# A two-layer transformer with a mixture of experts: work dealt anew over the turns, rounding on GpSimd, tiles fetched at loaded addresses, results scattered

## The reference

```
x  = x + attn0(ln(x)) + ffn0(ln(x))       # the same ln(x) feeds both
x  = x + attn1(ln(x)) + moe(ln(x))

attn:  16 heads of 8 features, softmax over 512 keys, output product (128 x 128)
ffn0:  h = silu(q(xn) @ q(wg)) * (q(xn) @ q(wu))      # 352 hidden features
       y = q(h) @ q(wd)
q(a):  blocks of 16: scale = max|a| / 6; round a / scale to 0 .5 1 1.5 2 3 4 6; times scale
moe:   g = softmax(relu(xn @ Wr1 + br1) @ Wr2 + br2); two best of 8 experts, weights softmax(g2 / 2)
       out = silu(xn @ Ws1 + bs1) @ Ws2 + bs2          # shared expert, 512 hidden features
       out += w_e * (silu(xn @ We1[e] + be1[e]) @ We2[e] + be2[e])   for the two experts e
```

## Time and profile before

| | |
|---|---|
| runs | 1662.01, 1664.07, 1670.28 us |
| profiled execution | 1662.64 us, span 1660.9 us |
| TensorE busy | 1199.5 us (72%), VectorE 1016.8 (61%), ScalarE 723.0 (44%), GpSimd 375.0 (23%) |
| mean granted TensorE clock | 0.868 |
| turns a1 to a7 | from 208.7 to 1278.5 us, with turns b between |
| last maxima with tiles beside them | 1323.7 to 1455.8 us |
| tiles alone | 1455.8 to 1564.1 us |
| last attention, then the end | 1564.1 to 1602.5, then to 1660.9 us |

### The profile page before, as it was taken

One profiled execution on the slowest core, in us unless ns is written; L12 is line 12 of the kernel. 1 busy time (PEld: TensorE's weight loads), 2 busy tenths in 40 slices (PEclk: granted clock), 3 DMA queues, 4 the chain that ended last, 5 costly groups with the idle time before them and its releaser, 6 DMA issues.

```text
span 1660.9 us, 18766 instructions
## 1 busy us (share of the span) xinstructions
PE 1199.5 (72%) x6747; PEld 522.3 (31%) x6807; DVE 1016.8 (61%) x1596; ACT 723.0 (44%) x921; POOL 375.0 (23%) x395
## 2 busy tenths in 40 slices
PE   2657478877786788777867887787778858888851
PEld 1113123212321332223212321232223246677510
DVE  7855677766676767666766676777685425411122
ACT  1045044644464446444644464446454713233450
POOL 5020111101110111011101110111001344455475
PEclk9668668987898889878987798889989979999985
DMA  4934232133313321432133213331410363455332
GB/s 135 349 149 115 89 99 83 30 111 82 85 30 107 95 76 30 112 94 73 29 109 85 84 30 106 80 86 30 113 34 14 96 159 122 131 149 163 110 104 69
DMA packets 143230, 159.65 MB, mean 96 GB/s; under 512 B 14585, under 2 KB 132546, under 8 KB 141090
## 3 DMA queue, kind: packets, MB, share of 16 engines
q1 hardware_dynamic: 129986, 123.87, 26.7%
q0 software_dynamic: 12208, 34.04, 6.9%
q10 hardware_dynamic: 944, 0.54, 0.1%
HBM read 90.11 MB, written 67.76 MB: 95 GB/s over the span
## 4 chain that ended last, share of the span: by engine, by line
PE 27%; DVE 27%; issue 21%; POOL 9%; ACT 6%; DVEq 6%; DMA 3%; SPq 1%; ACTq 0%; POOLq 0%
DVE nm L959 13%; PE sums L347 5%; ACT ex L695 3%; PE mx L359 3%; PE ring L458 3%; PE mx L329 3%; PE mx L409 2%; PE mx L449 2%; PE ring L433 2%; POOL qs L1361 2%; POOL ks L1361 2%; PE ring L253 2%; POOL xn L1313 2%; DVEq L914 1%; DVEq L873 1%
## 5 line engine op out<-in xcount | busy, mean ns | idle before, releaser
L695 ACT ACTIVATE ex<-mx 128x1024 f32<-128x1024 f32 x512 | 512.4, 1025 | 505.4 <-PE mx L359 503.0
L959 DVE TENSOR_REDUCE nm<-mx 128x2 f32<-128x1024 f32 x512 | 600.6, 1216 | 168.8 <-PE mx L329 165.5
L359 PE MATMUL mx<-qs,ks 74*128 74x512 bf16 (+1 forms) x964 | 316.9, 422 | 104.0 <-DMA qs<-nm_hl 52.6
L347 PE MATMUL sums<-ex,vs 128*18 128x512 f32 x2048 | 304.3, 669 | 5.0 <-ACT pv_sb L699 2.6
L329 PE MATMUL mx<-km,qm 32*128 32x512 bf16 x1024 | 151.5, 431 | 83.2 <-DVE nm L959 54.5
L359 PEld LDWEIGHTS mx<-qs,ks 128*128 128x128 bf16 (+1 forms) x1024 | 78.7, 102 | 404.3 <-issue 234.7
L1304 POOL TENSOR_TENSOR rstd<-veps,minus_half 128x4 f32<-128x4 f32 x16 | 16.6, 1038 | 561.3 <-DVE veps L865 561.3
L1340 POOL DMA_INDIRECT xsort<-xn,pos_i x64 | 62.7, 979 | 238.9 <-DVE pos_i L1046 221.8
L1331 POOL TENSOR_TENSOR parts<-qk_f,parts 128x512 bf16<-128x512 f32 x32 | 36.3, 1154 | 321.0 <-DVE parts L876 321.0
L329 PEld LDWEIGHTS mx<-km,qm 32*128 32x128 bf16 x1024 | 36.9, 93 | 222.4 <-DVE nm L959 97.3
L373 PE MATMUL ring<-ident,pv_sb 128*128 128x128 f32 x128 | 21.9, 298 | 59.1 <-DVE att L975 57.6
(11 more groups left out here) (211 smaller groups left out, 1613.8 us busy)
## 6 DMA issues: line engine op xcount, KB each, us to landing
scratch<-parts SPq DMA_DIRECT2D x128, 256.0 KB, 3.6
ks<-scratch SPq DMA_DIRECT2D x64, 256.0 KB
qs<-scratch SPq DMA_DIRECT2D x64, 256.0 KB
xsort<-hs SPq DMA_DIRECT2D x16, 1024.0 KB, 23.5
qm<-scratch SPq DMA_DIRECT2D x64, 128.0 KB, 2.6
km<-scratch SPq DMA_DIRECT2D x64, 128.0 KB, 2.6
rest<-parts SPq DMA_DIRECT2D x32, 128.0 KB, 3.4
ysort<-qs SPq DMA_DIRECT2D x20, 128.0 KB, 1.8
```

The costliest lines, as they stand in the source:

```text
L347: done = pe.matmul(acc[32 * j:32 * j + 2 * VW, :], values[:, start:start + 2 * VW], ex[:, s % NEX, j, :], start=q == 0 and t == 0, stop=q ...
L359: done = pe.matmul(bank[:, j, :], ks[l][r, h, t * P:(t + 1) * P], qs[l][r, h, :], start=True, stop=True)
L695: act.activation(ex[:, s % NEX, 2 * i:2 * i + 2, :], bank[:, :, :], ACT.Exp, scale=SCALE).then_inc(free, 1)
L959: dve.tensor_reduce(nm[l][:, t, h:h + 2], bank[:, :, :], AX.X, ALU.max, negate=True).then_inc(free, 1)
```

## The change

**A new dealing of the turns.** Many pieces of side work stand in other slots. On VectorE the layer norm statistics of batch b+2 (layer 0) stand in turn b(b) instead of a later turn a; GpSimd's `normalize(0, b+2)` goes with them. `split_qk` is cut in two pieces in two slots; so are the halves of the gates and of the shared expert's hidden product, which had shared a slot. The first half of h is quantised in turn b, the second in turn a. The rounding of x and h goes from VectorE to GpSimd (`round_x`, `round_h`). The high part of `max_rows` is copied by ScalarE. On SP `load_rows(0, b+1, 0)` goes ahead of layer 1's stores.

**Clearing.** `xsort` is cleared by 32 transfers of half the size, issued by ScalarE, one in each slot of turns a0 and b0.

**Tiles.** A row of `xsort` carries two more numbers: the token's number and its first expert. SP fetches weights and tokens by plain DMAs whose first row it loads from `w_row` and `x_row` into a register. VectorE works out, for each tile, where each result row belongs (`y_row`), and GpSimd scatters results by indirect DMA to `y2`, which is in the order of the tokens, one plane for a token's first expert and one for the second (rows of padding go to a region aside). The tiles start six slots later in the last turn (`FIRST_TILE`).

**The end.** `result_rows` is gone, and a batch's results come by two plain DMAs on SP instead of eight gathers.

The diff, cut to its core (the moved comparisons in `work_a` and `work_b` are given by those of VectorE):

```diff
@@ TensorE: tile_in; turn_a
-                pe.wait_ge(xg_in[i % 2], (i // 2 + 1) * 32)
+                pe.wait_ge(xg_in[i % 2], (i // 2 + 1) * 16)
...
-                    else:
-                        tile_step(k)
+                    elif k >= FIRST_TILE:
+                        tile_step(k - FIRST_TILE)
@@ ScalarE
+            def max_rows(l, b, half):
+                layer, batches = rows_before(l, b)
+                wait(act, rows_in[layer][half], batches * N_ROWS)
+                bank = from_ring(("m", l, b, half))
+                act.copy(nm_hl[:, half, 0, :], bank[0:NH // 2, :]).then_inc(high_ready, 1)
+            def clear_rows(i):
+                if i < NZERO:
+                    act.dma_start(xsort[i * ZR * P:(i + 1) * ZR * P, :].rearrange("(p r) c -> p (r c)", p=P),
+                                  hs[:, 0:3, :].rearrange("p c t -> p (c t)")[:, 0:ZR * XW]).then_inc(zero_out, 16)
@@ VectorE
-                if step == 2:
-                    quantize_round(dst, T).then_inc(xq_ready, 1)
...
             def max_rows(l, b, half):
-                layer, batches = rows_before(l, b)
-                wait(dve, rows_in[layer][half], batches * N_ROWS)
                 bank = from_ring(("m", l, b, half))
-                dve.tensor_copy(nm_hl[:, half, 0, :], bank[0:NH // 2, :])
-                dve.drain()
+                dve.wait_ge(high_ready, row_sets.at((l, b, half))[1] + 1)
                 dve.tensor_tensor(nm_hl[:, half, 1, :], ...)
...
             def tile_in(i):
                 bank = from_ring(("T", i))
                 dve.tensor_copy(xgT[i % 2], bank[:, 0:TS]).then_inc(ring_free, 1)
+                dve.tensor_scalar(plane[i % 2][:, :], xg[i % 2][:, :, P + 1], t_exp[:, i:i + 1], float(PLANE), ALU.not_equal, ALU.mult)
+                dve.scalar_tensor_tensor(no_token[i % 2][:, :], xg[i % 2][:, :, P], 0.0, aside[:, i, :], ALU.is_equal, ALU.mult)
+                dve.drain()
+                dve.tensor_tensor(plane[i % 2][:, :], plane[i % 2][:, :], xg[i % 2][:, :, P], ALU.add)
+                dve.drain()
+                dve.tensor_tensor(y_row[:, i, :], plane[i % 2][:, :], no_token[i % 2][:, :], ALU.add).then_inc(y_row_ready, 1)
@@ VectorE: work_a, work_b (places)
-                    for i in range(2):
-                        for step in range(3):
-                            if at == (1 + 3 * i + step + i, "c"):
-                                quantize_h(b, i, step)
+                    if at == (1, "c"):
+                        quantize_h(b, 1, 0)
+                    if at == (7, "c"):
+                        quantize_h(b, 1, 1)
-                    if at == (0, "c"):
-                        norm_stats(0, b + 1)
-                    if at == (4, "c"):
-                        split_qk(0, b + 1)
+                    if at == (3, "c"):
+                        split_first(0, b + 1)
+                    if at == (5, "c"):
+                        split_second(0, b + 1)
...
-                    if at == (12, "b"):
+                    if at == (15, "a"):
                         shared_out(b - 1)
...
+                if b + 2 <= LAST and at == (7, "c"):
+                    norm_stats(0, b + 2)
+                    if at == (13, "c"):
+                        quantize_h(b + 1, 0, 0)
+                    if at == (14, "c"):
+                        quantize_h(b + 1, 0, 1)
@@ GpSimd
+            def round_and_scale(d, n, qsc, done, count):
+                for op in (ALU.add, ALU.subtract):
+                    pool.tensor_tensor(d, d, binade[:, 0:n], op).then_inc(rounded, 1)
+                    pool.wait_ge(rounded, 2 * count + (1 if op == ALU.add else 2))
+                d3 = d.rearrange("p (k q) -> p k q", q=QB)
+                pool.tensor_tensor(d3, d3, per_block(qsc, n), ALU.mult).then_inc(done, 1)
...
-            def fetch_weights(i):
-            def fetch_tokens(i):
-            def fetch_results(b):
+            def scatter_results(i):
+                pool.wait_ge(y_row_ready, i + 1)
+                ring_read(pool, ("TO", i))
                 for h in range(2):
+                    pool.indirect_dma_start(out=y2[:, :], out_offset=bass.IndirectOffsetOnAxis(ap=y_row[:, i, h:h + 1], axis=0),
+                                            in_=yo[i % 2][:, h * P:(h + 1) * P], in_offset=None).then_inc(y_out[i % 2], 16)
@@ SP
+            def fetch_weights(i):
+                first = sp.value_load(w_row[0:1, i:i + 1], min_val=0, max_val=(E - 1) * P)
+                if i >= NW:
+                    sp.wait_ge(ring_full, ring.at(("TO", i - NW))[1] + 1)
+                sp.dma_start(wbuf[i % NW], wmoe[bass.ds(first, P), :]).then_inc(w_in[i % NW], 16)
+            def fetch_tokens(i):
+                first = sp.value_load(x_row[0:1, i:i + 1], min_val=0, max_val=ROWS - TS)
+                if i >= 2:
+                    sp.wait_ge(ring_full, ring.at(("T", i - 2))[1] + 1)
+                    sp.wait_ge(y_row_ready, i - 1)
+                sp.dma_start(xg[i % 2], xsort[bass.ds(first, TS), :].rearrange("(h p) c -> p h c", p=P)).then_inc(xg_in[i % 2], 16)
...
-            for i in range(NZERO):
-                sp.dma_start(xsort[i * 16 * P:(i + 1) * 16 * P, :].rearrange("(p r) c -> p (r c)", p=P),
-                             hs[:, :, :].rearrange("p c t -> p (c t)")).then_inc(zero_out, 16)
             load_rows(0, 0, 0)
...
+                if b + 1 <= LAST:
+                    load_rows(0, b + 1, 0)
                 store_early(1, b)
                 load_max(1, b)
                 store_late(1, b)
-                if b + 1 <= LAST:
-                    load_rows(0, b + 1, 0)
...
+            store_base(LAST - 1)
+            sp.wait_ge(tiles_ready, 1)
+            sp.wait_ge(scattered, 16 * 8 * B)
+            for i in range(NW - 2):
+                fetch_weights(i)
             for i in range(NTILE):
...
+                fetch_tokens(i)
+                if i + NW - 2 < NTILE:
+                    fetch_weights(i + NW - 2)
...
             for b in range(B):
+                for c in range(2):
+                    first = c * PLANE + 1 + b * T
+                    sp.dma_start(yb[b % 2][:, c, :, :], y2[first:first + T, :].rearrange("(t p) c -> p t c", p=P)).then_inc(yb_in[b % 2], 16)
```

More of the change, by code:

```diff
@@ L35 @@
 ROWS = E * CAP
-NZERO = ROWS // (16 * P)
+XW = P + 2
+ZR = 8
+NZERO = ROWS // (ZR * P)
+PLANE = B * T + 1
+FIRST_TILE = 6
 TS = 256
@@ L87, in two_layers @@
 def two_layers(nc, x, w_qkv, w_out0, b_out0, w_gate, w_up, w_down, wqT, wkT, wvT, woT, bq, bk, bv, bo,
-               wr1, br1, wr2, br2, w1s, b1s, w2s, wmoe, b2, scratch, rest, xsort, ysort, base, out):
+               wr1, br1, wr2, br2, w1s, b1s, w2s, wmoe, b2, scratch, rest, xsort, y2, base, out):
     ctx = ExitStack()
@@ L335, in max_rows @@
                     pair_read(pe, ("M", l, b, u, i))
+                row_sets.take((l, b, half))
                 transpose_tiles(("m", l, b, half), lambda t: nm[l][:, t, half * 8:half * 8 + 8], cols=NH // 2)
@@ L633, in _ @@
             turn_a(B)
-            for i in range(SLOTS, NTILE + 1):
-                if i == SLOTS:
+            for i in range(SLOTS - FIRST_TILE, NTILE + 1):
+                if i == SLOTS - FIRST_TILE:
                     max_rows(1, LAST, 1)
@@ L796, in turn_a @@
                     work_a(b, k, "b")
-                    if b > LAST:
-                        tile_hidden(k)
+                    if b == 0:
+                        clear_rows(k)
+                    if b > LAST and k >= FIRST_TILE:
+                        tile_hidden(k - FIRST_TILE)
             def turn_b(b):
@@ L831, in _ @@
             turn_a(B)
-            for i in range(SLOTS, NTILE):
+            for i in range(SLOTS - FIRST_TILE, NTILE):
+                if i == SLOTS - FIRST_TILE:
+                    max_rows(1, LAST, 1)
                 tile_hidden(i)
@@ L934, in quantize_h @@
                 if step == 0:
+                    wait(dve, xq_ready, b + 1)
+                    wait(dve, h_ready, 2 * b + i - 1)
                     dve.drain()
-                    quantize_scales(h, 2 * F0)
+                    quantize_scales(h, 2 * F0, qsc[i])
                 if step == 1:
-                    quantize_binades(h, h, 2 * F0)
-                if step == 2:
-                    quantize_round(h, 2 * F0).then_inc(h_ready, 1)
+                    wait(dve, h_ready, 2 * b + i)
+                    quantize_binades(h, h, 2 * F0).then_inc(h_scaled, 1)
             def ffn_up(b, i):
@@ L1076, in tile_table @@
                 dve.drain()
-                dve.tensor_tensor(shift[:, :], ends[:, :], tiles[:, :], ALU.subtract)
                 dve.tensor_tensor(after[:, :, :], each(iota_t), over(ends), ALU.is_ge)
                 dve.drain()
-                dve.scalar_tensor_tensor(shift[:, :], shift[:, :], float(TS), ebase[:, :], ALU.mult, ALU.subtract)
                 dve.tensor_reduce(t_exp[:, :], after[:, :, :], AX.X, ALU.add)
```

(7 more changed lines are left out.)

306 lines of the change are left out of this document (160 added, 146 removed).

## The result

The changed kernel took 1759.91 us (median of four runs from 1756.90 to 1766.92), the kernel before 1663.04 beside it: a ratio of 1.058 [1.053, 1.064] (a 95% interval stands in square brackets, here and below), so slower, as forecast (1725, range 1605 to 1800). Its profiled execution took 1756.90 us with a span of 1755.2, 94.3 more than before.

A forecast was written before the change was run, and what follows sets the result against it. In the layers neither VectorE nor TensorE is full and both wait; tiles alone are TensorE bound. Span 1660.9 - 92 (turns, clearing) + 192 (tiles) - 38 (end) = 1723, so 1725 us for the run, range 1605 to 1800.

The forecast's parts named there:

- The tiles: Expert tiles: tokens queued behind waiting weights, so the whole fetch stands in each of 36 steps of 10.6 us; 192 us more.
- L: Tiles: length of the exposed fetch, from SP's wake to the tokens' landing; 4.2 us, bounds 3.2 and 5.2.
- V: Tiles: SP's load of a row number into a register, part of the exposed fetch; taken as 0.5 us.
- The end: After the last attention: two plain transfers replace eight gathers a batch, combining fits beside the last attention; 37.6 us less.
- The turns and the clearing: Layers: 101 us from the turns plus 3 from clearing, less 9 for GpSimd holding VectorE; rounded down to 92 less.
- The tokens are now ready a turn early, so 4.7 goes too.: Turn a: TensorE's wait for GpSimd's normalised tokens disappears; 4.7 us a turn.
- 30.8 becomes 17.0.: Turn a: VectorE's work besides its maxima falls as rounding (7.3 us) and statistics, scaling and copies (6.5) leave.
- 51.2 + 17.0 + 6.2 + 3.3 + 4: Turn a: maxima slots, VectorE's other work, shared expert wait, second table loads, small waits; 81.7 us instead of 96.8.
- rival (2): GpSimd holds VectorE in the turns (50 us more), or TensorE's clock never returns in the tiles (58 more): 1780; chance 0.15.
- (1): Tiles: the fetch is short and TensorE keeps the higher clock level, steps of 7.2 us: 1603 us; chance 0.27.
- S: Tiles: length of one step, exposed fetch 4.2 plus TensorE's part 6.4; 10.6 us, bounds 7.2 and 13.
- (3): Tiles: SP gets ahead and a step hides the fetch as before, steps of 4.7 us: 1510 us; chance 0.05.

The follow-up runs named there:

- tok1: Changed kernel with SP asking for tokens of tile i+1 ahead of weights of tile i+2, one TensorE step before use: 1570.69 us.
- tok2: Changed kernel with SP fetching tokens and weights of the same tile in pairs, tokens first, two TensorE steps before use: 1563.55 us.
- swap: Changed kernel with row numbers loaded ahead of the wait for the weights' buffer, and behind that wait tokens sent before weights: 1637.99 us.
- norm: Changed kernel with GpSimd normalising batch b+2 right after layer 1's residual, ahead of the rounding of h: 1753.74 us.
- rnd: Kernel with `tok2` and `norm` edits together (1543.14 us), rounding of x and h back on VectorE, each step in its own slot: 1553.65 us.
- pair: Kernel with `tok2` and `norm` edits together (1543.14 us), both halves of the shared expert's silu in one slot again, likewise the gates': 1495.29 us.
- rows: `pair` with the first rows of maxima for the next turn a sent behind layer 1's stores on SP again: 1554.91 us.
- warm: Kernel with `tok2` and `norm` edits together (1543.14 us), score products repeated in five places of turns a1 to a7: 1529.49 us.

## Why the prediction was right, and where it was not

**The tiles (192 forecast, 184 measured)** were read rightly from the code's order: what is queued on SP behind a transfer that waits for TO(i-2) is what TensorE needs next, as `tok1` and `tok2` show. The step was 10.6 forecast and 10.38 measured, the wait 4.2 and in most tiles 4.2 to 4.6, TensorE's part 6.4 and 6.0. The clock's part of it, taken from one tile, held in many tiles of the stage: H of 2.8 to 3.6. Two things in it were luck. 36 steps of 10.6 (382) came out as 35 of 10.38 (363), and the rest, put at 51, took 61 (the first fetch, put at 4, was awaited for 12.1): the two misses cancel in part. And L came out right although its parts were mis-sized: the register load V, taken as 0.5, shows 0.80 less some 0.25 and costs nothing, since the tokens land behind the weights anyway; the weights ahead, taken as 0.5, cost most of the 2 us by which `swap` shortened the wait.
**The end (38 forecast, 37.4 measured)**: batches 0 to 6 are combined by 1732.83, just before the last attention ends at 1733.7 (batch 7's own sum, 2.35 us, stands behind it, as in the kernel before), and from the division to the last store it takes 9.8 us, to the end 9.2 more.

```profile
1730.48 2.35 DVE L1168 SCALAR_TENSOR_TENSOR qs<-qs,tg 128x128 f32<-128x128 f32 x8 [1.59 <-DMA qs<-base]
1736.23 0.36 DVE L1016 RECIPROCAL rden<-ring 128x32 f32<-128x32 f32 x1 [3.40 <-PE ring L385]
1746.01 0.38 SPq L1546 DMA_DIRECT2D out<-macc  x1
```

**The turns and the clearing (92 forecast, 52 measured)** are where the sum failed, by 40 us; the tiles gave 8 of that back, and 1725 fell 35 short of 1759.9. Turn a2 fell from 96.8 to 92.5, not to 82; a7 from 81.5 to 79.6. The prediction's own sign of being wrong, turns a above 90, came true in a2 to a6. Three steps failed:
- "The tokens are now ready a turn early, so 4.7 goes too." The statistics were early, the normalising was not: on GpSimd it had been put behind the rounding, and the price of the rounding looked only at the readers of h, not at what is queued behind it. TensorE waited 34.2 us in six turns. With the order mended (`norm`) the wait went, and 6 to 20 us came of it.
- "30.8 becomes 17.0." The passes left as forecast, but VectorE's busy time in turn a2 fell by 8.0 us, not by 13.8: beside GpSimd's rounding one pass took 1.67 us instead of 0.16, and beside `third_part` a cast took 0.65 instead of 0.18 and a copy, new in this kernel, 1.03 (0.17 in turn a7, where GpSimd has no such work). `rnd` shows that VectorE's work was not what set the turn.
- "51.2 + 17.0 + 6.2 + 3.3 + 4": the turn as a sum of VectorE's work and waits. Its fit to the turn of before proved little, for in the changed kernel VectorE's work could be raised by 4.5 us (`rnd`), or the wait for tokens taken out (`norm`), with no change of turn a3. What slot 0 gains in `norm`, slots 1, 2 and 7 give back at a clock of 0.85, 0.66 and 0.80, where it was 0.97, 1.00 and 1.00. The row said so: 74.3 of 96.8 us busy at a clock of 0.83.

Smaller slips of the sum: the 6.6 us for the rows of maxima and the 4.7 for the tokens are means that take in the waits ahead of the turns (11.3 before a0, which the clearing counts again, and 10.0 at the start); in the turns alone they were 5.9 and 4.0 to 4.5. 95 was set down as 92, the end was reckoned from 1603.5 where the earlier trace rows has 1602.5, and in rival (2) the clock's price of 1.6 a step should be 7.8 - 6.4 = 1.4. None of them decides anything.

**What held in the turns:** the second pair of table loads (46 forecast, 48 in `pair`), the queue move of SP (the rows are no longer awaited; 46 forecast if undone, 60 in `rows`), GpSimd's hold on VectorE in the rounding alone (0.9 to 1.5 a batch; 1.4 to 1.5 in one pass). The clearing's part (3 forecast) is too small to be told.

**The rivals:** (1) came nearest in `swap`, with S from 6.2 to 8, 1638 us. (2) did not happen as one thing, yet the clock took back in the turns a part of what the forecast had counted as gain. (3), a hidden fetch, needed the other order of SP's list: 1563 measured, 1510 forecast. What stays open is how the loss in turn a is split between waiting for the bank `ring`, for VectorE's maxima and the clock, and what brings the clock down in one slot and not in another; `warm` got back 14 us in the median and 29 in the profiled execution.

## What to carry to other kernels

An engine that issues transfers in order makes every transfer behind a waiting one as late as that one: ask of each wait what stands behind it and who needs that next, and put the transfer with the earliest reader ahead (196 us for two lines here). The same question holds for an engine that is given another's work: ahead of turn a2 the rounding of half of h took GpSimd 4.8 us, and TensorE stood 5.84 us for what was queued behind it. And where the profile shows a stage at a clock under 1, a wait is not worth its length: in the tiles 153 us of waiting taken out gave 196, for the clock came back; in the turns 34 gave 6 to 20, for the clock fell in other slots.

## What the hardware showed unasked

- A token transfer of 130 KB was used 2.23 us after its issue when it went first, and 3.13 to 3.48 us when 514 KB of weights had been issued on the same queue just before it.
- TensorE's first product was at the higher level in about two of three tiles after waits of 2.4 us (1.89 us) and at the lower level, or partly so, after waits of 4.3 (2.78 to 3.62).
- 38 products added to turn a3 (8 us of work at the higher level) made it 9 us shorter: the clock of slots 0 and 2 went from 0.71 and 0.66 to 1.00.
- A VectorE pass on 128x4 elements with two inputs took 1.54 us beside GpSimd's rounding and 0.16 without it; a copy of 128x4 took 1.03 beside `third_part` and 0.17 without. The maxima kept their 1.22 us.
